# Decoder kernel, cross attentions: who multiplies the exponentials by the reciprocal sums, and a new order table

## What is computed

```python
x = _layernorm(x + _L0_attn_ref(...))    # mamba: selective scan, 256 channels x 16 states
x = _layernorm(x + _L0_xattn_ref(...))   # cross attention, 32 context tokens, 16 heads
x = _layernorm(x + _L0_ffn_ref(...))     # 8 experts, top 2, and a shared one
x = _layernorm(x + _L1_attn_ref(...))    # windowed attention, 16 heads
x = _layernorm(x + _L1_xattn_ref(...))   # cross attention again, 16 heads
x = _layernorm(x + _L1_ffn_ref(...))     # two layers of local attention and gated FFN
```

```python
scores = jnp.einsum('bqhd,bkhd->bhqk', q * SCALE, k)
attn = jax.nn.softmax(scores, axis=-1)
out = jnp.einsum('bhqk,bkhd->bqhd', attn, v).reshape(B, SQ, INNER)
```

## Time and profile before

| | us |
|---|---|
| median of 3 runs (lowest to highest) | 1656.91 (1656.44 to 1661.01) |
| the profiled execution, its own time | 1651.61 |
| its span, first to last instruction | 1649.8 |
| busy: PE / DVE / ACT / POOL | 1377.5 / 1080.7 / 835.1 / 326.7 |
| mean granted TensorE clock | 0.91 |

### The profile page before, as it was taken

The page is one execution under the profiler, slowest core; times in us unless marked ns, Lnnn a source line. Parts: engine busy times, 40 slices in busy tenths (PEclk is TensorE's granted clock), DMA queues, the critical chain, the costliest instruction groups (busy, mean ns, idle before and its releaser), DMA issues. The chain is left out here.

```text
span 1649.8 us, 23108 instructions
## 1 busy us (share of the span) xinstructions
PE 1377.5 (83%) x8604; PEld 862.6 (52%) x8604; DVE 1080.7 (66%) x2223; ACT 835.1 (51%) x2060; POOL 326.7 (20%) x212
## 2 busy tenths in 40 slices
PE   6877679998899788888875777899989987878885
PEld 3522236676666446546631223567756654654662
DVE  5789975115787777467447998711378878745853
ACT  3265426432765256665647552353357635665652
POOL 0136520002000042032001664100110004302400
PEclk9779978999999889998977888999999998999997
DMA  5500000000000010000000000000000000100000
GB/s 206 211 32 1 0 1 26 1 0 1 1 1 2 10 36 20 1 20 14 8 13 13 0 1 0 14 14 1 0 1 2 2 1 14 27 1 14 20 8 13
DMA packets 12928, 30.90 MB, mean 19 GB/s; under 512 B 1425, under 2 KB 5905, under 8 KB 12562
## 3 DMA queue, kind: packets, MB, share of 16 engines
q1 hardware_dynamic: 8978, 23.14, 3.8%
q10 hardware_dynamic: 3840, 6.29, 1.7%
HBM read 17.89 MB, written 5.24 MB: 14 GB/s over the span
## 5 line engine op out<-in xcount | busy, mean ns | idle before, releaser
L840 POOL TENSOR_TENSOR scratch<-scratch 128x1024 f32<-128x1024 f32 x64 | 150.0, 2353 | 197.3 <-DVE scratch L807 175.1
L659 PE MATMUL psum<-scratch,w_const 128*128 128x512 f32 x256 | 152.8, 730 | 23.3 <-POOL scratch L840 23.3
L1015 ACT ACTIVATE scratch<-psum,w_experts 128x512 f32<-128x512 f32 x144 | 98.2, 687 | 136.5 <-PE psum L971 133.3
L565 POOL TENSOR_SCALAR rstd<-mv 128x4 f32<-128x4 f32 x28 | 7.2, 258 | 786.6 <-DVE mv L552 786.6
L807 DVE TENSOR_TENSOR_SCAN scratch<-psum,scratch 128x512 f32<-128x512 f32 x128 | 151.3, 1210 | 13.9 <-ACT psum L732 13.3
L995 PEld LDWEIGHTS psum<-expert_weights,scratch 128*128 128x128 f32 x1152 | 134.7, 192 | 19.4 <-issue 18.9
L971 PE MATMUL psum<-xT,expert_weights 128*128 128x512 f32 x288 | 136.2, 606 | 1.0 <-ACT scratch L1015 1.0
L995 PE MATMUL psum<-expert_weights,scratch 128*128 128x128 f32 x1152 | 136.1, 275 | 0.6 <-DVE y L1060 0.5
L1060 DVE SCALAR_TENSOR_TENSOR y<-psum,comb,y 128x128 f32<-128x128 f32 x128 | 36.0, 344 | 146.0 <-PE psum L995 146.0
L1499 ACT ACTIVATE scratch<-psum,mx 128x128 f32<-128x128 f32 x256 | 90.1, 374 | 73.1 <-DVE mx L1590 73.0
L732 ACT ACTIVATE psum<-scratch,a_neg 128x512 f32<-128x512 f32 x128 | 87.9, 690 | 77.1 <-DVE scratch L807 60.0
(11 more groups left out here) (229 smaller groups left out, 3067.9 us busy)
## 6 DMA issues: line engine op xcount, KB each, us to landing
scratch<-scratch ACTq DMA_DIRECT2D x48, 128.0 KB, 2.3
expert_weights<-in_expert_weights SPq DMA_DIRECT2D x9, 512.0 KB, 9.5
folded_products<-expert_weights SPq DMA_DIRECT2D x8, 512.0 KB, 3.6
folded<-folded_products SPq DMA_DIRECT2D x8, 512.0 KB, 3.4
w_local<-in_local SPq DMA_DIRECT2D x1, 3122.0 KB
scratch<-in_cross SPq DMA_DIRECT2D x1, 2624.5 KB, 12.8
x<-in_x SPq DMA_DIRECT2D x4, 256.0 KB, 3.1
out<-xT SPq DMA_DIRECT2D x4, 256.0 KB, 2.4
```

The source lines that it names most:

```text
L659: ins = pe.matmul(sum_banks[c], ident, t.m.hC[:, 2 * ((n - 1) % 2) + c, :], start=(n == 1), stop=(n == NS))
L840: t.eng.tensor_tensor(t.m.hC[:, 2 * (n % 2):2 * (n % 2) + 2, :], t.m.hs[:, n % 2], C, ALU.mult)\
L1015: act.activation(t.m.hid[:, k % 2, f, :], t.a.take(), ACT.Gelu_apprx_tanh, bias=W("experts", "b1")[:, c:c + 1]).then_inc(t.s["a_freed"], 1)
```

## The change

The product L927 leaves DVE. The reciprocal now raises a new semaphore `rinv_ready`; POOL waits for that, makes the same product with the same tiles and raises `prob_ready`. `cross_pool` has its four products between `norm_pool` calls. There are 32 products, four in each of eight cross attentions. All four lists of `TURNS` are new (their rows tell a reader nothing; one is shown). Nothing else differs: each other instruction is issued as often as before, except ACT's table reloads, which follow from the order: 55 before, 41 now.

```diff
@@ TURNS
     "pool": [
-        4, 2, 6, 1, 1, 1, 1, 1, 1, 1, 1, 1, 1, 1, 1, 1, 1, 1, 1, 1, 1, 4, 2, 1, 2, 6, 2, 2, 2, 2, 2, 2, 2, 2, 2,
+        3, 2, 4, 1, 1, 1, 1, 1, 1, 1, 1, 1, 1, 1, 1, 1, 1, 1, 1, 1, 1, 1, 1, 1, 1, 1, 1, 4, 4, 3, 1, 1, 3, 1, 1,
...
@@ own_names
-                     "max_ready vx_loaded ss_ready root_ready rope_ready sq_ready rst_ready hn_ready "
+                     "rinv_ready max_ready vx_loaded ss_ready root_ready rope_ready sq_ready rst_ready hn_ready "
@@ cross_vector
                     yield from t.w.step(dve.tensor_reduce(t.m.sums[:, j, 0:H1], heads(t.m.e1[:, j, :]), X, ALU.add))
-                    yield from t.w.step(dve.reciprocal(t.m.rinv[:, j, 0:H1], t.m.sums[:, j, 0:H1]))
-                    e = heads(t.m.e1[:, j, :])
-                    dve.tensor_tensor(e, e, wide(t.m.rinv[:, j, 0:H1]), ALU.mult).then_inc(t.s["prob_ready"], 1)
+                    dve.reciprocal(t.m.rinv[:, j, 0:H1], t.m.sums[:, j, 0:H1]).then_inc(t.s["rinv_ready"], 1)
                     t.skip(a=1)
@@ cross_pool
         def cross_pool(t, inner):
             if inner:
                 yield from norm_pool(t)
+            for i in range(NT):
+                yield
+                t.w(t.s["rinv_ready"])
+                e = t.m.e1[:, i % 2, :].rearrange("p (h k) -> p h k", h=H1)
+                by = t.m.rinv[:, i % 2, 0:H1].rearrange("p (h o) -> p h o", o=1).to_broadcast([P, H1, S])
+                t.eng.tensor_tensor(e, e, by, ALU.mult).then_inc(t.s["prob_ready"], 1)
             yield from norm_pool(t)
             t.skip(a=1 + NT, v=NT, o=1)
 
```

## The result

The changed kernel is faster: 1629.66 us (median of 4 runs, 1628.73 to 1630.91) against 1658.13 (4 runs, 1656.44 to 1661.01), ratio 0.9827 with a 95% interval of 0.981 to 0.9845. (In the experiments further down the kernel before took 1638 to 1673 us, with medians of 1658 to 1663 by group of runs, and with the mean granted clock at 0.917 near 1640, 0.910 near 1657 and 0.894 near 1672. The 95% intervals of the ratios there are 5 to 9 us wide to either side, so lengths of stages are used beside them.)

A forecast was written before the change was run, and what follows sets the result against it. No engine is full over the whole: PE bounds the experts, DVE is busiest in the scans, PE in the local layers. Terms -1.1 + 7 + 0.5 - 3 - 1 + 1 give +3.4 us, 1660 on the median, range 1638 to 1680.

The forecast's parts named there:

- The start: First pass's start: setup matmuls first, lane 0's first scan some 15 us later, DVE's work the same; 0, up to +5.
- The product on POOL: In the crosses: 1.18 us per product, bounds 0.69 and 3.0, hidden in a 2.4 us tile.
- rival C: Crosses: product costs more than 1.18 us, by its own length or by holding up DVE; slower, 1673, chance 0.07.
- my +1 for contention: Pairs of crosses: POOL's products hold up the other lane's normalizing L557, 1.2 us a hit, one or two hits: +1.
- The pairs of crosses: Second crosses: tile period falls from 2.68 to 2.3 to 2.4 us, PE late next; -3 for each pass's pair.
- perhaps -1: First crosses: less to give, a round trip in the first pass; the second pass's, now a pair, save perhaps -1.
- The change of pass: Between passes: first scan at 897, lane 1's preparation moved ahead of the scans, +0.9; table reloads -2; scans end at -1.1.
- The head start of the experts: Second pass: in step, both crosses follow the scans and PE's early expert work is lost; +7, at most 10.
- A: Faster: joining the lanes costs nothing, relief comes in full; first scan of second pass before 890; -20, 1637, chance 0.32.
- B: Slower: second pass's scans don't shorten, lanes in step wait for the round trip; last scan after 1025; 1677, chance 0.21.

The follow-up runs named there:

- e2_pool_old_table: The kernel before with only the product moved to POOL, its order on PE, ACT and DVE kept: 1653.9 us, ratio 0.9983 to the kernel before.
- e3_new_start: Product on POOL, new order up to the first pass's window stage, the kernel before's order from there: 1638.6 us, ratio 0.9898 to the kernel before.
- the repeated one: The changed kernel measured once more, no edit: 1636.0 us, ratio 0.9868, 22 us under the kernel before.
- the experiment: The changed kernel with its second pass's crosses apart, in the first pass's order, beside the unedited changed kernel: 1631.7 against 1636.2 us.
- the pair's profile: Profile of the changed kernel run on one chip beside its version with the second pass's crosses apart: 1636.2 against 1631.7 us.

## Why the prediction was wrong

**The start: the step that failed.** I costed it at 0 "with up to +5" and it gave -19.7 in the first two profiles and 15 us by the medians of `e2_pool_old_table` and `e3_new_start`. The prediction says that DVE "has the same work before the end of both scans", which is true, and takes from it that the end stays put. But DVE was idle 40 of the first 216.4 us in the profile before and 29.4 of 196.7 after; the work was never the bound of the whole stretch. I had taken 0 to 74 us as one window and not cut it at 40 to 60 us, where PE is busy 20.00 of 20 us at a clock of 0.52. That row alone says that this part of the start hangs on PE and its clock. I also put lane 0's first scan at 80 us, from 62.0; it came at 67.0, since this time the setup ran at full clock, and lane 1's came at 97.3 instead of 115.7. Against the old order at full clock, whose first scan came at 51.3, the delay is 15.7 us: my 15 us were right for a start that the profile before did not have. With -19.7 in place of the 0 the sum would have given 1640, 10 us above the first comparison and 4 above the repeated one.

**The product on POOL** was sized well: 1.05 us against 1.18. That it would bound a tile or hold up DVE (rival C) did not happen; the DVE instructions that ran beside it kept their lengths, and none of the normalizing ones met it, so my +1 for contention was 0. In the old order five norms did meet it, at 0.7 us each. For DVE's work with both inputs in SBUF, however, the prediction's nearest row could not speak: none of the L927 stood beside one of POOL's large products. Other lines of the same profile did. A DVE product of 128x1024 with both inputs in SBUF takes 1.22 us; the three that began well inside a product L840 took 2.48, 2.48 and 1.60, and ended about 1.1 us after it. The first:

```profile
108.99 2.35 POOL L840 TENSOR_TENSOR scratch<-scratch 128x1024 f32<-128x1024 f32 x1 [6.53 <-DVE scratch L807]
...
109.94 2.48 DVE L788 TENSOR_TENSOR scratch<-scratch 128x1024 f32<-128x1024 f32 x1
```

That part of rival C did not come all the same: the crosses have no such large DVE instruction left, and the add, which reads PSUM, kept to 0.69 us.

**The pairs of crosses.** For the second crosses I forecast -3 each. By the product's move within the new order it was -2.2 and -1.8; from before to after the two pairs changed by -1.8 and +1.7. The 2.3 to 2.4 us a tile that I took from PE's rows was not the limit: the steady tiles went down to 1.98 us, DVE's time in full. The pair gained less than eight such tiles would give, because its first and last tiles wait for PE (2.65 us before one of them). For the first crosses I forecast "perhaps -1" in one of the two passes; it was -5.3 and -5.6 by the same comparison. Both were mis-sized. I took the tile of one lane alone for a round trip that the product's move can't shorten, and DVE's queue was in it (3.72 to 3.39 us a tile); and I gave the second pass's pair, now in step, -1 where eight tiles lost 0.7 us each. Together the move gave 14.9 us where my terms for it were 7.

**The change of pass.** The last FFN product of the lanes' local layers ended at 821.9, where I had 834.7 and, with the start's 20 taken off, 815; the first scan came at 874.5 (897 less 20: 877), the last at 984.6 (1016 less 20: 996). The mechanism, that lane 1's preparation moves ahead of the scans and lanes in step lose nothing much there, was right in its direction, and the stretch was better than my +0.9 us by some 10: between first and last scan 110 us instead of 119.

**The head start of the experts.** Forecast +7, and PE's first expert matmul would begin about 9 us after lane 0's did before. Crosses and experts together gave +6.1 in the first profiles and +2.5 by the experiment. Right in sign; by the experiment, which alone sets the head start apart, hardly half the size. What I had nothing for is the window stage behind it: +10.3 in the first profile and 8.3 by the experiment, at a clock of 0.96 in the pair's profile, against 0.99 in the version with the crosses apart.

**The rivals.** A, the faster one, had the sign, but its mechanism was the change of pass ("a first scan before 890"). The scan at 874.5 meets the words of that test, but it leads the 882.1 of before by less than the 20 us that the start had given. B and C did not occur. The range failed because every case shared the zero for the start; its bounds were made from the terms that I had sized, and none from the one that I had waved through. The repeated comparison, 22 us instead of 28, would also have fallen below it, near 1635.

## What to carry to other kernels

When an order is made anew, compare the two orders in every stage, and read each stage's bound from small windows before a term is set to zero; a stretch in which PE is busy all the time at half clock is the first suspect. An operation that moves to an idle engine is worth what the order makes of it: here nothing that could be told in the old one and about 15 us in the new. And where lanes run in step, look at the stage behind: what one stage gains by it the next may pay. And when an order is undone in parts, give every engine's list the same part, or the part tested is another one.

## What the runs showed of the hardware

Between 40 and 60 us, PE's clock was 0.52 and 0.64 in two executions of the kernel before, and 0.94 and 0.95 in two kernels with the same start; where PE was the bound, that was 10 us of 1650. In one group of runs the mean clock and the time of the kernel before went together, from 1640 us at 0.917 to 1664 at 0.901. A 128x512 product of exponentials with a broadcast reciprocal took 1.046 to 1.051 us on GpSimd and 0.656 to 0.693 on VectorE, and VectorE's own two-input additions beside it stayed at 0.69 us. The Trainium skill, "GPSIMD Engine Reference", section 4.1, calls GpSimd about 2x slower for such work; here it was 1.5x. For products of 128x1024 it was 1.9x in this case too (2.35 us on GpSimd, one operand repeated once along the row, against 1.22 for VectorE's of two full operands). A VectorE product of that size with both inputs in SBUF, 1.22 us alone, took 2.48 us when it began during such a GpSimd product, and a group of four normalizing instructions, 1.11 us alone, took 1.83 beside a GpSimd product of 1.05.
